# A state-space layer on one core: each pair of states scanned by one instruction of 1024 columns instead of two of 512

## The chip, the core and the metric

One of the eight cores of a Trainium2 chip runs the whole program. Its engines are TensorE (PE, matrix products, with a separate row PEld for its weight loads), VectorE (DVE), ScalarE (ACT), GpSimd (POOL) and SyncE (SP, which here issues the DMAs). Each engine works through its own list of instructions in order and stops at a semaphore until another engine has raised it. The metric is the device time of one execution in microseconds (us), median of the runs.

## What is computed

Two layers follow each other on an input of 2 sequences, 2048 positions, 512 features, in float32. The first is a conditional Mamba layer, the second a linear attention layer. The change lies in the scan of the first:

```
xz = in_proj(layernorm(x) * (1 + scale) + shift);  x_in, z = split(xz)      # 1024 channels each
u  = silu(causal_conv4(x_in));  dt_r, B, C = split(x_proj(u));  dt = softplus(dt_proj(dt_r))
for each position t, channel d, state n (16 of them):
    h[d,n] = h[d,n] * exp(dt[t,d] * A[d,n]) + (dt[t,d] * u[t,d]) * B[t,n]
    y[t,d] = sum_n h[d,n] * C[t,n]
y = (y + u * D) * silu(z);  x = x + gate * out_proj(y)
```

## The kernel before

**Tiling.** The 2 x 2048 positions are cut into 8 chunks c of 512 positions. The 1024 channels are cut into 8 tiles j of 128. A chunk and a tile make a unit, U = 8c + j, 64 of them; a unit has 16 states, so there are 1024 steps s = 16U + pr, with pr the state from 0 to 15. Two neighbouring states make a pair, G = s // 2, 512 of them; g = G % 8 is the pair's place in its unit. The scan runs along the 512 positions, in columns, and is one VectorE instruction for a state.

**The path of one pair.** (1) ACT computes the decays exp(dt * A) of a state (`exps`), 512 columns, into one of four PSUM banks, DA[s % 4]. (2) VectorE, or GpSimd for the pairs in `POOLED`, multiplies dt*u by the B of both states into a buffer hb of 2 x 512 columns (`expand`). Six such buffers go round (R = 6), and an expand waits until TensorE has read the pair six before (semaphore p_y). (3) VectorE scans each state in place (`scan`, line 1094): it waits for the state's decays (a_da) and for the expand (v_tt or g_ex), and counts v_sc up when it is done. (4) ACT copies the pair's last column where a later chunk needs it (`keep_state`), and GpSimd multiplies both states by C (line 1529). (5) TensorE adds up the states over transposed matmuls into PSUM (`nsum`, line 368).

**The order.** All of it is written out by hand: each engine runs a loop over the 1024 steps, and tables say at which (tile j, state pr) an engine puts in the work that belongs to other places: the next unit's softplus ('soft': pr 6 on ACT, behind a copy of the last unit's sums at the same pr 6, `y_copy`), the product with silu(z) (`y_fin`, pr 11 on VectorE), the next chunk's projections, convolution and silu, the last chunk's output projection. ACT runs three steps ahead: in its step s it first does what the tables put there and then `exps(s + 3)`. That call waits until the bank that it overwrites has been scanned, `e.wait_ge(v_sc, s - 3)` in terms of its own s. VectorE's order in an even step is `expand` of the next pair, then the scan of the first state; the second state's scan follows in the odd step. A softplus and a silu each need an activation table of their own, which is loaded by ACT (lines 654 and 890 around a silu, 654 and 754 around a softplus).

**Pooled pairs.** By the tables `EACH` and `OWN`, 114 of the 512 expands are GpSimd's. In the units up to U = 62, where ACT puts in a softplus, the pairs g = 4 and g = 5 are both VectorE's in 42 units, and one of the two is GpSimd's in 21 (mostly j = 2, 6 and 7). In the units with j = 4, one of the pairs g = 1 and g = 2 is GpSimd's; there ACT has a silu of z and one of u at pr 0.

After the 1024 steps the second layer follows, which the change doesn't touch.

## Time and profile before

| | |
|---|---|
| median of 3 runs | 2237.83 us (2236.24 to 2241.0) |
| profiled execution, its own time | 2238.82 us |
| span of the profile | 2237.0 us |
| stretch of the scans, 69 to 1747 us | 1678 us: DVE busy 1642, POOL 1593, PE 1500, ACT 1370 |
| before it and after it | 69 us and 490 us |
| mean granted TensorE clock | 0.974 |

A busy time is the sum of an engine's records. Records of VectorE and ACT overlap a little: the next one begins before the one ahead has ended, so that the distance from start to start, called the pitch here, is shorter than the duration, and it is the pitch that an instruction costs when the queue is full.

### The profile page before, as it was taken

The page shows a single profiled execution, that of the slowest core. Times are in us where ns is not written, and L with a number is a line of the kernel's source. Part 1 is how long each engine was busy: PE and PEld are TensorE (multiplying, and loading weights), DVE is VectorE, ACT ScalarE, POOL GpSimd, SP SyncE. Part 2 cuts the span into 40 slices and gives each one's busy share as a digit, 9 for nine tenths or more (in the row PEclk, how much of TensorE's full clock was granted, in tenths as well). Part 3 has the DMA queues.
Part 4 walks back from the last instruction along what each step waited for, and adds up shares of the span by engine and source line. Part 5 has one row for each costly group of instructions (what it writes and reads, how often), then busy time and mean ns, then how long its engine had stood idle before and what let it go on. Part 6 is the DMA issues. An engine that isn't in the chain of part 4 may idle for free.

```text
span 2237.0 us, 31435 instructions
## 1 busy us (share of the span) xinstructions
PE 2040.1 (91%) x10240; PEld 1320.8 (59%) x10240; DVE 1985.6 (89%) x2245; ACT 1674.5 (75%) x3186; POOL 1744.8 (78%) x1139
## 2 busy tenths in 40 slices
PE   8889989988998999899989988999868899999999
PEld 3355555545555554555555555545545688888878
DVE  4899999989999999999999999999999766666666
ACT  3688797878887888888887889887677455466655
POOL 0599999999999999999999999999999422232225
PEclk9899999999999999999999999999988999999999
DMA  6623342352234143434342351334001211111113
GB/s 219 240 83 95 97 165 67 85 171 85 76 98 176 57 104 81 175 99 99 107 149 66 86 191 56 84 93 179 29 29 55 99 34 36 37 53 62 41 57 132
DMA packets 122592, 220.73 MB, mean 99 GB/s; under 512 B 24317, under 2 KB 39933, under 8 KB 122430
## 3 DMA queue, kind: packets, MB, share of 16 engines
q1 hardware_dynamic: 122430, 218.74, 31.5%
q8 instruction: 82, 1.34, 0.2%
q14 instruction: 80, 0.66, 0.1%
HBM read 171.91 MB, written 17.30 MB: 85 GB/s over the span
## 4 chain that ended last, share of the span: by engine, by line
PE 44%; issue 15%; DVE 14%; POOL 11%; ACT 11%; DMA 3%; SPq 1%; DVEq 0%; POOLq 0%; ACTq 0%
PE ps L516 15%; DVE arena L1094 9%; PE ps L297 9%; POOL arena L1529 8%; PE ps L368 6%; DVE arena L1082 5%; PE ps L358 3%; ACT arena L654 3%; ACT ps L654 3%; PE ps L344 2%; ACT L654 2%; POOL arena L1493 2%; PE ps L324 2%; ACT L754 1%; PE ps L510 1%
## 5 line engine op out<-in xcount | busy, mean ns | idle before, releaser
L1529 POOL TENSOR_TENSOR arena<-arena 128x1024 f32<-128x1024 f32 x512 | 1199.8, 2362 | 97.3 <-ACT arena L654 93.8
L1094 DVE TENSOR_TENSOR_SCAN arena<-ps,arena 128x512 f32<-128x512 f32 x1024 | 1189.3, 1202 | 13.0 <-ACT ps L654 12.0
L654 ACT ACTIVATE ps<-arena 128x512 f32<-128x512 f32 x1087 | 713.2, 677 | 207.7 <-DVE arena L1082 105.6
L368 PEld LDWEIGHTS ps<-keep,arena 128*128 128x128 f32 x4096 | 475.0, 144 | 311.0 <-POOL arena L1529 170.7
L368 PE MATMUL ps<-keep,arena 128*128 128x128 f32 x4096 | 540.8, 281 | 117.9 <-POOL arena L1529 100.0
L1082 DVE TENSOR_TENSOR arena<-ps,arena 128x1024 f32<-128x1024 f32 x398 | 476.7, 1198 | 22.4 <-PE ps L368 18.2
L297 PE MATMUL ps<-arena 128*128 128x512 f32 x1024 | 469.2, 600 | 12.4 <-issue 11.5
L297 PEld LDWEIGHTS ps<-arena 128*128 128x128 f32 x1024 | 188.0, 192 | 229.4 <-issue 228.9
L1493 POOL TENSOR_TENSOR arena<-arena 128x1024 f32<-128x1024 f32 x114 | 269.3, 2362 | 17.2 <-PE ps L368 17.1
L358 PE MATMUL ps<-arena 128*128 128x512 f32 x512 | 238.1, 601 | 1.7 <-DVE arena L1115 1.7
L654 ACT ACTIVATE arena<-ps 128x512 f32<-128x512 f32 (+2 forms) x330 | 168.4, 526 | 77.4 <-PE ps L297 58.2
L654 ACT ACTIVATE arena<-arena 128x2 f32<-128x2 f32 (+6 forms) x678 | 190.8, 300 | 27.3 <-DMA arena<-scr_bc 14.6
L1541 POOL TENSOR_TENSOR arena_c<-arena_c 128x512 f32<-128x512 f32 x32 | 33.4, 1044 | 161.6 <-DVE arena_c L1253 160.4
L358 PEld LDWEIGHTS ps<-arena 128*128 128x128 f32 x512 | 96.1, 196 | 104.4 <-issue 99.8
L654 ACT ACT_TABLE_LOAD x121 | 155.2, 1283 | 2.9 <-PEq L1857 0.7
L324 PE MATMUL ps<-arena 128*64 128x512 f32 x448 | 112.5, 624 | 27.5 <-DMA arena<-arena 27.3
L1423 POOL TENSOR_SCALAR arena_b<-arena_b 128x2 f32<-128x2 f32 x32 | 7.4, 231 | 143.9 <-DVE arena_b L1104 143.7
L654 ACT ACTIVATE arena_c<-arena_c 128x256 f32<-128x256 f32 (+3 forms) x112 | 54.9, 493 | 85.9 <-POOL arena_c L1541 59.4
L654 ACT ACTIVATE arena_b<-ps,keep 128x256 f32<-128x256 f32 x128 | 70.9, 554 | 50.4 <-PE ps L510 41.0
L1213 DVE TENSOR_TENSOR xl<-arena_b,xh 128x256 fp32r<-128x256 f32 x128 | 57.6, 467 | 45.4 <-ACT xh L654 44.6
L1463 POOL TENSOR_TENSOR arena<-arena 128x511 f32<-128x511 f32 (+1 forms) x63 | 80.1, 1272 | 14.4 <-ACT arena L654 11.4
L654 ACT ACTIVATE arena_b<-arena_b 128x512 f32<-128x512 f32 x64 | 48.5, 806 | 50.4 <-POOL arena_b L1428 50.4
(153 smaller groups left out, 2683.4 us busy)
## 6 DMA issues: line engine op xcount, KB each, us to landing
arena<-in_inT SPq DMA_DIRECT2D x184, 256.0 KB, 2.8
arena<-scr_bc SPq DMA_DIRECT2D x80, 512.0 KB, 10.0
arena<-arena SPq DMA_DIRECT2D x224, 128.5 KB, 2.4
arena<-scr_bc SPq DMA_DIRECT2D x48, 511.0 KB, 9.5
arena<-in_x SPq DMA_DIRECT2D x17, 512.0 KB, 3.7
scr_x<-arena SPq DMA_DIRECT2D x32, 256.0 KB, 2.0
arena_b<-scr_x SPq DMA_DIRECT2D x16, 512.0 KB, 3.6
arena_c<-scr_x SPq DMA_DIRECT2D x32, 256.0 KB, 2.9
```

The source lines that it names most:

```text
L297: last = e.matmul(P, W[:, q, :], xnT[c % 2][:, q, :], start=(q == 0), stop=(q == 3))
L324: last = e.matmul(P[64 * h:64 * h + 64, :], W[:, 2 * h + p, 0:64], xt[:, h, 2 * p:2 * p + T], start=(p == 0), stop=(p == 1))
L358: e.matmul(P, u[c % 2][:, q, 128 * n:128 * n + 128], wout[:, q, :], start=(c == NCH - 1 and q == 0 or parts and q == 6), stop=(q == 7 or p ...
L368: last = e.matmul(YP[:, 128 * q:128 * q + 128], hb[G % R][:, i, 128 * q:128 * q + 128], ident, start=(g == 0 and i == 0 and q == 0), stop= ...
L516: last = e.matmul(P, lhs(a, k), rhs(b, k), start=(k == 0 and n == 0), stop=(k == 3 and n == 2))
L654: return e.activation(o_, i_, f, **kw)
L1082: e.tensor_tensor(hb[G % R], DU.unsqueeze(1).broadcast_to([128, GN, T]), Bt[:, GN * g:GN * g + GN, :], MUL).then_inc(v_tt)
L1094: e.tensor_tensor_scan(H, DA[s % 4], H, 0.0, MUL, ADD).then_inc(v_sc)
L1213: e.tensor_tensor(lo[:, f, :], f_bufs[i % 3], hi[:, f, :].bitcast(f32), SUB).then_inc(v_lo)
L1463: e.tensor_tensor(spt[:, lo:T], dt[U % 2][:, lo:T], u[c % 2][:, j, lo:T], MUL).then_inc(g_du)
L1493: e.tensor_tensor(hb[G % R], spt.unsqueeze(1).broadcast_to([128, GN, T]), Bt[:, GN * g:GN * g + GN, :], MUL).then_inc(g_ex)
L1529: e.tensor_tensor(H, H, Ct[:, GN * g:GN * g + GN, :], MUL).then_inc(g_w)
```

## The change

The four decay banks become one PSUM tensor of 4 x 512 columns, so that two neighbouring banks can be read as one row of 1024. A pair's scan is now one instruction (`joint`) over 1024 columns of decays and of hb. So that the second state doesn't start from the last value of the first, the first column of every second bank is set to zero once, at the start (semaphore a_z0), and the decays of odd states are written from column 1 on. A product with zero then cuts the chain; the exact decay of that first column was never used, since the state starts at zero (later chunks add the kept state through B's first column). `JOINT` holds all 64 places, so no pair is left scanned in two. "Slots kept" in the words of the change means that the tables of places, the four banks and the waits of `exps` stay as they are.

```
-        PS = [ctx.enter_context(nc.psum_tensor(f"ps{i}", [128, 512], f32))[:, :] for i in range(8)]
+        decay = ctx.enter_context(nc.psum_tensor("ps_da", [128, 4, 512], f32))
+        PS = [decay[:, i, :] for i in range(4)] + [ctx.enter_context(nc.psum_tensor(f"ps{i}", [128, 512], f32))[:, :] for i in range(4, 8)]
...
+        JOINT = {(0, 0), (0, 1), (0, 2), (0, 3), (0, 4), (0, 5), (0, 6), (0, 7), (1, 0), (1, 1), (1, 2), (1, 3), (1, 4),
...
                 if s >= 4:
                     e.wait_ge(v_sc, s - 3)
-                act(DA[s % 4], dt[U % 2], ACT.Exp, scale=An[:, U % 8, n:n + 1]).then_inc(a_da)
+                lo = s % 2
+                act(DA[s % 4][:, lo:T], dt[U % 2][:, lo:T], ACT.Exp, scale=An[:, U % 8, n:n + 1]).then_inc(a_da)
...
             e.wait_ge(a_A, 2)
+            act(decay[:, 1::2, 0], zero3[:, 0:2], ACT.Identity).then_inc(a_z0)
             exps(0)
...
             def scan(s):
                 U, n = divmod(s, 16)
                 c, j = divmod(U, 8)
-                H = hb[(s // 2) % R][:, s % 2, :]
-                e.wait_ge(a_da, s + 1)
+                joint = (j, n // 2) in JOINT
+                if s == 0:
+                    e.wait_ge(a_z0, 1)
+                e.wait_ge(a_da, s + 2 if joint else s + 1)
...
-                e.tensor_tensor_scan(H, DA[s % 4], H, 0.0, MUL, ADD).then_inc(v_sc)
+                H = hb[(s // 2) % R]
+                if joint:
+                    e.tensor_tensor_scan(flat(H), flat(decay[:, s % 4:s % 4 + 2, :]), flat(H), 0.0, MUL, ADD).then_inc(v_sc, 2)
+                else:
+                    e.tensor_tensor_scan(H[:, s % 2, :], DA[s % 4], H[:, s % 2, :], 0.0, MUL, ADD).then_inc(v_sc)
...
             expand(0)
-            scan(0)
...
-                if s:
+                if s % 2 == 0 or (j, pr) not in JOINT:
                     scan(s)
```

On VectorE, unit 40 from its pair g = 4 to its pair g = 6 stood so before. The rows of line 1082 are expands (of g = 5, 6 and 7), those of line 1094 scans, and line 1115 is `y_fin`:

```order
L1082 TENSOR_TENSOR arena<-ps,arena 128x1024 [waits p_y,g_E0,d_B5]
L1094 SCALAR_TENSOR_TENSOR arena<-ps,arena 128x512 [waits v_tt,a_da] x2
L1082 TENSOR_TENSOR arena<-ps,arena 128x1024 [waits p_y,g_E0,d_B6]
L1094 SCALAR_TENSOR_TENSOR arena<-ps,arena 128x512 [waits v_tt,a_da]
L1115 TENSOR_TENSOR arena<-ps,arena 128x512 [waits a_sz,p_yb]
L1094 SCALAR_TENSOR_TENSOR arena<-ps,arena 128x512 [waits v_tt,a_da]
L1082 TENSOR_TENSOR arena<-ps,arena 128x1024 [waits p_y,g_E0,d_B7]
```

Now the same place reads so; line 1090 is the expand, 1106 the joint scan, 1129 `y_fin`:

```order
L1090 TENSOR_TENSOR arena<-ps,arena 128x1024 [waits p_y,g_E0,d_B5]
L1106 SCALAR_TENSOR_TENSOR arena<-ps_da,arena 128x1024 [waits v_tt,a_da]
L1090 TENSOR_TENSOR arena<-ps,arena 128x1024 [waits p_y,g_E0,d_B6]
L1106 SCALAR_TENSOR_TENSOR arena<-ps_da,arena 128x1024 [waits v_tt,a_da]
L1129 TENSOR_TENSOR arena<-ps,arena 128x512 [waits a_sz,p_yb]
L1090 TENSOR_TENSOR arena<-ps,arena 128x1024 [waits p_y,g_E0,d_B7]
```

Two scans have become one, whose wait on a_da now counts both states, and `y_fin` has moved from between the two scans of pair g = 5 to behind the joint one.

On ACT, the softplus of unit 40 stood so before. The rows that write ps and wait on v_sc are `exps` (of states 7, 8 and, last, 9), 128x2 is `keep_state`, the row that waits on p_y is `y_copy`, the one on p_dt the softplus:

```order
L654 ACTIVATE ps<-arena 128x512 [waits v_sc] x2
L654 ACTIVATE arena<-arena 128x2 [waits v_sc]
L654 ACTIVATE ps<-arena 128x512 [waits v_sc]
L654 ACTIVATE arena<-ps 128x512 [waits p_yb,p_y]
L654 ACT_TABLE_LOAD [waits g_du]
L654 ACTIVATE arena<-ps 128x512 [waits p_dt]
L754 ACT_TABLE_LOAD
L654 ACTIVATE ps<-arena 128x512 [waits v_sc]
```

And now:

```order
L660 ACTIVATE ps_da<-arena 128x512 [waits v_sc]
L660 ACTIVATE ps_da<-arena 128x511 [waits v_sc]
L660 ACTIVATE arena<-arena 128x2 [waits v_sc]
L660 ACTIVATE ps_da<-arena 128x512 [waits v_sc]
L660 ACTIVATE arena<-ps 128x512 [waits p_yb,p_y]
L660 ACT_TABLE_LOAD [waits g_du]
L660 ACTIVATE arena<-ps 128x512 [waits p_dt]
L760 ACT_TABLE_LOAD
L660 ACTIVATE ps_da<-arena 128x511 [waits v_sc]
```

Nothing on ACT has moved: the four instructions still stand between the exponentials of states 8 and 9. Only the odd states are one column shorter. The waits on v_sc keep their numbers, but v_sc now goes up by two at the end of a pair.

## Rows read from the trace of the kernel before

**Rows 1.** Windows: busy time of each engine in the stretch of the scans.

```profile
69.00:1747.00 1678.00, 1500.47 (x6809) 877.67 (x6808) 1642.46 (x1499) 1369.77 (x2558) 1593.25 (x900) 0.97 0.34 105
```

**Rows 2.** VectorE's groups by line, in that stretch: busy, mean ns; idle before.

```profile
L1094 DVE TENSOR_TENSOR_SCAN arena<-ps,arena 128x512 f32<-128x512 f32 x1024 | 1189.3, 1202 | 13.0 <-ACT ps L654 12.0
L1082 DVE TENSOR_TENSOR arena<-ps,arena 128x1024 f32<-128x1024 f32 x397 | 475.5, 1198 | 19.0 <-PE ps L368 18.2 <-POOL arena L1483 0.7
L1115 DVE TENSOR_TENSOR arena<-ps,arena 128x512 f32<-128x512 f32 x63 | 42.0, 666 | 3.5 <-PE ps L381 3.5
```

**Rows 3.** Waits of ACT for VectorE: us in total, times, longest.

```profile
ACT ps L654 <- DVE arena L1082: 105.6, 53, 3.8
ACT ps L654 <- DVE arena L1094: 99.4, 138, 2.6
```

**Rows 4.** Timeline of VectorE, unit 40: start, us, instruction.

```profile
1128.86 2.33 DVE L1094 TENSOR_TENSOR_SCAN arena<-ps,arena 128x512 f32<-128x512 f32 x2
1131.11 1.20 DVE L1082 TENSOR_TENSOR arena<-ps,arena 128x1024 f32<-128x1024 f32 x1
1132.22 2.33 DVE L1094 TENSOR_TENSOR_SCAN arena<-ps,arena 128x512 f32<-128x512 f32 x2
1134.47 1.20 DVE L1082 TENSOR_TENSOR arena<-ps,arena 128x1024 f32<-128x1024 f32 x1
1135.58 2.32 DVE L1094 TENSOR_TENSOR_SCAN arena<-ps,arena 128x512 f32<-128x512 f32 x2
...
1140.07 0.66 DVE L1115 TENSOR_TENSOR arena<-ps,arena 128x512 f32<-128x512 f32 x1
1140.66 1.21 DVE L1094 TENSOR_TENSOR_SCAN arena<-ps,arena 128x512 f32<-128x512 f32 x1
```

**Rows 5.** Timeline of ACT at the softplus of unit 40.

```profile
1130.11 0.69 ACT L654 ACTIVATE ps<-arena 128x512 f32<-128x512 f32 x1 [1.35 <-DVE arena L1094]
1131.20 0.60 ACT L654 ACTIVATE arena<-ps 128x512 f32<-128x512 f32 x1 [0.40 <-PE ps L368]
1131.82 1.28 ACT L654 ACT_TABLE_LOAD   x1
1133.11 0.60 ACT L654 ACTIVATE arena<-ps 128x512 f32<-128x512 f32 x1
1133.72 1.28 ACT L754 ACT_TABLE_LOAD   x1
1135.02 0.69 ACT L654 ACTIVATE ps<-arena 128x512 f32<-128x512 f32 x1
1135.65 0.57 ACT L654 ACTIVATE arena<-arena 128x2 f32<-128x2 f32 x3
```

**Rows 6.** Timeline of VectorE at the softplus of unit 47, where g = 5 is GpSimd's.

```profile
1316.07 3.44 DVE L1094 TENSOR_TENSOR_SCAN arena<-ps,arena 128x512 f32<-128x512 f32 x3
1320.28 1.22 DVE L1094 TENSOR_TENSOR_SCAN arena<-ps,arena 128x512 f32<-128x512 f32 x1 [0.77 <-ACT ps L654]
```

**Rows 7.** Timeline of ACT at the same place: the exponential of state 9.

```profile
1319.56 0.69 ACT L654 ACTIVATE ps<-arena 128x512 f32<-128x512 f32 x1
```

**Rows 8.** Timeline of ACT at the silu of unit 44 (j = 4), between states 2 and 3.

```profile
1226.68 1.28 ACT L654 ACT_TABLE_LOAD   x1
1227.97 0.60 ACT L654 ACTIVATE arena<-ps 128x512 f32<-128x512 f32 x1
1228.46 1.05 ACT L654 ACTIVATE arena<-arena 128x1024 f32<-128x1024 f32 x1
1229.53 1.28 ACT L890 ACT_TABLE_LOAD   x1
1230.83 0.69 ACT L654 ACTIVATE ps<-arena 128x512 f32<-128x512 f32 x1
```

**Rows 9.** Timeline of VectorE at that place: pairs 6, 7, an expand, pairs 0, 1.

```profile
1222.49 4.55 DVE L1094 TENSOR_TENSOR_SCAN arena<-ps,arena 128x512 f32<-128x512 f32 x4
1226.97 1.20 DVE L1082 TENSOR_TENSOR arena<-ps,arena 128x1024 f32<-128x1024 f32 x1
1228.08 4.69 DVE L1094 TENSOR_TENSOR_SCAN arena<-ps,arena 128x512 f32<-128x512 f32 x4
```

More of the change, by code:

```diff
@@ L139, in program @@
             ("ft", "q", "v", "k", "qt", "kt", "kv", "ya", "o"))
-        a_sc, a_A, a_row, a_no, a_xn, a_xh, a_hi, a_e0, a_xq, a_ue, a_du, a_su, a_xd, a_sp, a_sz, a_da, a_st, a_dg, a_x1, a_sm, a_sq = (
-            sem("a_" + n) for n in ("sc", "A", "row", "no", "xn", "xh", "hist", "e0", "xq", "ue", "du", "su", "xd", "sp", "sz",
+        a_z0, a_sc, a_A, a_row, a_no, a_xn, a_xh, a_hi, a_e0, a_xq, a_ue, a_du, a_su, a_xd, a_sp, a_sz, a_da, a_st, a_dg, a_x1, a_sm, a_sq = (
+            sem("a_" + n) for n in ("z0", "sc", "A", "row", "no", "xn", "xh", "hist", "e0", "xq", "ue", "du", "su", "xd", "sp", "sz",
                                     "da", "st", "dg", "x1", "sm", "sq"))
@@ L1159, in _ @@
                     expand(s // 2 + 1)
-                if s:
+                if s % 2 == 0 or (j, pr // 2) not in JOINT:
                     scan(s)
```

4 rows, old and new, of the table JOINT are left out of this document.

## The prediction

> **What bounds the kernel now.** I read the windows first. In the stretch of the scans VectorE is busy for 1642 of 1678 us, GpSimd for 1593, TensorE for 1500, ACT for 1370 [rows 1]. Records overlap a little, so none of these is quite a queue's load, but the order is clear: VectorE sets the pace, GpSimd follows at 95%, ACT has 18% to spare. VectorE's groups by line say what it does there: 1024 scans, 397 expands, 63 `y_fin`; and how little it waits: 12.0 us for decays from ACT, 18.2 and 3.5 us for TensorE, in 1678 [rows 2]. What VectorE is made to do or to wait for therefore lands in the time almost whole. ACT, in turn, waits some 205 us for VectorE in 191 places [rows 3]. The view ascribes about half of it to the expand, but by the program these are `exps`, which wait for a scan to free their bank. So ACT is on average ahead. The timelines show where it is not: at its bursts of table loads.
>
> **What the change takes away.** VectorE's queue gives the price from start to start. Two scans and what lies between them cost 1131.11 - 1128.86 = 2.25 us, an expand of 1024 columns 1.11 us, `y_fin` with 512 columns 0.59 us [rows 4]. The last two are the same operation with one operand in PSUM, so 512 columns cost 0.52 us and what is paid once for an instruction is 1.11 - 1.04 = 0.07 us. Taking that for the scan too, the joint scan costs 2.25 - 0.07 = 2.18 us, and 512 pairs save 36 us. The trace holds no scan of 1024 columns and none across two banks. Bounds: if the second bank or the longer row costs what the merging saves, 2.25 and a gain of 0. At the other end, if the fixed part is all by which a scan's record of 1.202 us [rows 2] exceeds twice 0.52 us, it is 0.16 us, and 82 us are saved. I take 0.07, the nearest row.
>
> The page "VectorE: DVE Perf Modes" of the Trainium skill (section on the TRN2 errata) gives a PSUM-source instruction 120 cycles beside one per element, and says that "a single large tile pays it once". At its 0.96 GHz that would be 0.125 us a pair and 64 us in all, an estimate from that page; the pitch in the rows shows 0.07 us of it, since the queue begins the next instruction before the last has ended.
>
> **What it adds: two banks come free at once, and two must be full at once.** Before, the first state's bank was free a scan earlier than the second's, and the second state's decays were needed a scan later than the first's. Now `exps` of both states of a pair wait for the end of the joint scan two pairs back, and both must be done before the next joint scan on those banks starts. From that end to that start VectorE does an expand, a joint scan and an expand: 1.11 + 2.18 + 1.11 us, less the 0.08 us by which records overlap (2.33 of 2.25), 4.32 us. With one of the expands on GpSimd it is 3.21 us. Within it ACT must do two exponentials and all that the tables put between them.
>
> *The softplus.* At pr 6 the tables put four instructions between the exponentials of states 8 and 9: `y_copy`, a table load of 1.28 us, the softplus, a table load of 1.28 us, from 1131.20 to 1135.02, 3.82 us [rows 5]. The need is 0.05 us from a scan's end (1128.86 + 1.20) to the exponential at 1130.11, 0.63 us for that one (the pitch of 1135.02 to 1135.65), 3.82, 0.69 for the second and 0.03 to the scan: 5.22 us. In the 42 units in which both expands are VectorE's, pair 4 starts 5.22 - 4.32 = 0.90 us late; in the other 21, 5.22 - 3.21 = 2.01 us. Unit 47 shows the second case without a model: the exponential of state 9 ended at 1319.56 + 0.69 = 1320.25 [rows 7], where the scan of state 8 had begun at 1316.07 + 2 x 1.12 = 1318.31 and that of state 9 waited until 1320.28 [rows 6]. A joint scan could not have begun before 1320.28, 1.97 us later than the scan of state 8 did. Together 42 x 0.90 + 21 x 2.01 = 80 us.
>
> *The silu at j = 4, pr 0.* From 1226.68 to 1230.83 ACT is at table loads and two silus, 4.15 us, between states 2 and 3 [rows 8]. The need is 0.05 + 0.63 + 4.15 + 0.69 + 0.03 = 5.55 us. Between pair 7 of the unit before and pair 1 VectorE has one expand and one joint scan (pairs 6 and 7, an expand, pairs 0 and 1 [rows 9]): 3.21 us. Late by 2.34 us in 7 units; in the last chunk, without the silu of u (1.05 us), by 1.29. Together 18 us.
>
> *Other bursts.* Where a burst stands before an even state, ACT meets it while it would wait anyway, and nothing is lost. I didn't walk every place. Units with j = 1, 5 and 6 have further silus, statistics and evacuations within a pair; I allow each of these 24 units one plain lateness of 0.9 us, 22 us, an estimate and the weakest term.
>
> *What takes some of it back.* 12.0 us of waiting for ACT is there already [rows 2] and is part of the 120. VectorE's 22 us of waits for TensorE [rows 2] shrink when it comes later anyway; I take half, 11 us, between 0 and 22.
>
> **What costs nothing.** `y_fin` moves behind the joint scan, one scan later in its unit; its input is rarely late (3.5 us in all [rows 2]) and now less so. Odd exponentials are one column shorter. The one zeroing instruction stands at the start, before the decays that ACT has ready ahead of the first expand. GpSimd, `keep_state` and TensorE wait for the end of a pair as before, and come 36 us sooner or with the late pairs later. SP's queue is untouched, and so is everything after 1747 us.
>
> **The sum.** 80 + 18 + 22 - 12 - 11 = 97 us of waits, less 36 us saved: 61 us more on 2238.82 us, the profiled execution's own time, which stands 1 us above the median of the runs. On the median that is 2299 us, 2.7% slower.
>
> **The rivals.**
> *ACT is far enough ahead, and only the saving remains.* For it: ACT's 205 us of waits for VectorE. Against it: those waits lie outside the bursts, and rows 6 and 7 show a decay ready after the scan ahead of it had begun. It decides where what stands between two exponentials is shorter than 4.32 - 1.40 = 2.92 us (1.81 with a GpSimd expand), and it is 3.82. Then the time would be 2238 - 36 = 2202 us. Chance 0.07.
> *Another queue sets the pace, so that neither term is seen.* GpSimd is at 95% and TensorE at 89% [rows 1]. Then VectorE would be waiting for freed buffers; it does so for 18 us [rows 2], so at most that much could be hidden or kept from it. About 2238 us. Chance 0.04.
> *The fixed part of an instruction is larger*, as a scan's record, not its pitch, would have it: 82 us saved, windows 0.09 us shorter at some 95 places (9 us lost): 2299 - 46 + 9 = 2262 us. The pitch in rows 4 speaks against it. The page of the Trainium skill named above speaks for a part of it: by its 64 us the time would be about 2276 us, an estimate. Chance 0.12.
> *Nothing is taken back and the joint scan saves nothing.* A late joint scan delays GpSimd's multiplication, TensorE's sums and with them the next expands; with a joint scan of 2.25 us the windows grow by 0.07 us (7 us less late): 2238 + 120 - 12 - 7 = 2339 us. For it: GpSimd has only 85 us of slack. Against: six buffers go round. Chance 0.12.
> The forecast itself, 2275 to 2325 us, has 0.65.
>
> **How the numbers follow.** The likeliest case gives 2299 us. The range goes from 2258 us, a little under the case of the larger fixed part, to 2335 us, nearly the worst case; it leaves out the first two rivals and the tails of the others. A measurement of this kernel tells 0.2% from no change, 4.5 us. Faster 0.07, the same 0.04, slower 0.89.
>
> **What the next profile would show.** 512 scans with a pitch of 2.18 us (2.1 to 2.25) in VectorE's timeline, and VectorE's busy time lower by some 60 us, since records overlap. VectorE waiting for ACT at line 1106 about 105 us in some 110 places, where it was 12 us in 25; the longest of about 2 us, in the units with j = 2, 6 and 7 at pair 4 and with j = 4 at pair 1, and of about 0.9 us at pair 4 of the others. ACT's waits for VectorE about as long as before. The stretch of the scans about 1740 us long, and 490 us behind it. The prediction is wrong if ACT's waits for VectorE stand within a pair, ahead of the burst, or if the pitch of the joint scan is far from 2.18 us; and its size is wrong if places other than pairs 4 and 1 hold most of the waiting.

## The result, and the profile after

The change made the kernel slower, as forecast, but by more: 2341.42 us, median of 4 runs (2337.99 to 2342.04), against 2237.83 us before. The ratio is 1.046 [1.0447, 1.0472], 104 us, where 61 us were forecast. The time stands 6 us above the upper end of the range. The profiled execution took 2341.62 us, its span is 2339.8 us.

The windows of the changed kernel, in the stretch of the scans (columns as in [rows 1]):

```profile
67.00:1849.00 1782.00, 1537.29 (x6805) 888.00 (x6806) 1622.53 (x987) 1382.13 (x2558) 1596.17 (x899) 0.95 0.32 99
```

The stretch is 1782 us long instead of 1678; what follows it has kept its 490 us. All of the loss lies here. VectorE is busy 20 us less than before (1622.53, before 1642), yet the stretch is 104 us longer: it waits. (The view counts overlapping records once, so a busy time is less than the sum of the records that was named ahead: 1024 scans of 1.202 us make 1231 us, where [rows 2] has 1189.3.) Its groups by line, in the same stretch, say for whom:

```profile
L1106 DVE TENSOR_TENSOR_SCAN arena<-ps_da,arena 128x1024 f32<-128x1024 f32 x512 | 1161.2, 2278 | 127.5 <-ACT ps_da L660 82.7 <-issue 44.5
L1090 DVE TENSOR_TENSOR arena<-ps,arena 128x1024 f32<-128x1024 f32 x397 | 476.7, 1201 | 31.6 <-PE ps L374 31.5
L1129 DVE TENSOR_TENSOR arena<-ps,arena 128x512 f32<-128x512 f32 x63 | 41.9, 665 | 0.2 <-PE ps L387 0.2
```

Beside [rows 2]: the scans wait 127.5 us where they waited 13.0 us; the expands wait 31.6 us for TensorE where it was 19.0; only `y_fin` waits less, 0.2 us for 3.5. Of the scans' waits 44.5 us are marked "issue", a wait for which the view names no releaser. The timeline shows what they are. VectorE in unit 40, from pair 3 to the expand behind pair 4:

```profile
1193.72 2.27 DVE L1106 TENSOR_TENSOR_SCAN arena<-ps_da,arena 128x1024 f32<-128x1024 f32 x1
1195.92 1.20 DVE L1090 TENSOR_TENSOR arena<-ps,arena 128x1024 f32<-128x1024 f32 x1
1197.04 2.27 DVE L1106 TENSOR_TENSOR_SCAN arena<-ps_da,arena 128x1024 f32<-128x1024 f32 x1
1199.23 1.20 DVE L1090 TENSOR_TENSOR arena<-ps,arena 128x1024 f32<-128x1024 f32 x1
1201.24 2.29 DVE L1106 TENSOR_TENSOR_SCAN arena<-ps_da,arena 128x1024 f32<-128x1024 f32 x1 [0.81 <-issue]
1203.45 1.20 DVE L1090 TENSOR_TENSOR arena<-ps,arena 128x1024 f32<-128x1024 f32 x1
```

and ACT between the exponentials of states 8 and 9 of that unit:

```profile
1196.03 0.69 ACT L660 ACTIVATE ps_da<-arena 128x512 f32<-128x512 f32 x1 [1.88 <-DVE arena L1106]
1196.66 0.58 ACT L660 ACTIVATE arena<-ps 128x512 f32<-128x512 f32 x1
1197.26 1.28 ACT L660 ACT_TABLE_LOAD   x1
1198.55 0.60 ACT L660 ACTIVATE arena<-ps 128x512 f32<-128x512 f32 x1
1199.17 1.28 ACT L760 ACT_TABLE_LOAD   x1
1200.46 0.69 ACT L660 ACTIVATE ps_da<-arena 128x511 f32<-128x511 f32 x1
```

The joint scan that begins at 1193.72 frees both banks at its end. 0.04 us later, at 1196.03, ACT begins to fill them, and the burst of the tables stands between the two exponentials, as in [rows 5]. The second one ends at 1201.15 and the joint scan of pair 4 begins at 1201.24. VectorE had nothing else from 1200.43 on. From freeing to scanning it is 5.25 us (the prediction had 5.22). The lateness in the row is 0.81 us; counted as the prediction counts, from where the scan would have begun with the usual overlap of 0.08 us, it is 0.89 us (0.90). So a wait marked "issue" here is a wait for ACT all the same, as the end of the exponential just ahead of the scan shows.

ACT in turn waits far longer for the scans, and TensorE longer ahead of line 303. Rows of the changed kernel's waits (engine, line, waited for: us in total, times, longest):

```profile
ACT ps_da L660 <- DVE arena L1106: 266.7, 257, 4.7
...
ACT ps L660 <- DVE arena L1090: 55.7, 55, 1.6
...
PE ps L303 <- issue: 30.5, 12, 3.8
```

The same wait of TensorE before, where the line was 297:

```profile
PE ps L297 <- issue: 11.5, 8, 2.1
```

The first row of [rows 3] is not `exps`, as the prediction took it to be. ACT has a second write into PSUM that waits for VectorE, `du_copy`, the copy of the next unit's dt*u, which waits until the last expand of its unit has read the old one. It writes ps in both kernels, and the exponentials of the changed kernel write ps_da, so the rows above keep the two apart: `du_copy` waits 55.7 us (105.6 before), the exponentials 266.7 us (99.4 before).

Walked record by record, from the end of the instruction ahead to the start of each scan, the waits for decays rose from 16.5 to 137.6 us (+121). Waits of the expands and of `y_fin` rose together from 25.3 to 33.8 us (+8.5). A pair in two scans took 2.245 us from start to start where nothing waited (the median; [rows 4] have 2.25 twice). The joint scan takes 2.197 us (2.20, 2.19 and 2.21 in the rows of unit 40 above). So merging saves 0.048 us a pair, 25 us in all. 121 + 8.5 - 25 = 104.5 us, and from the first scan's start to the last one's end the trace has 1781.5 instead of 1677.9 us, +103.6. The expectations below reckon with 2.235, 2.182 and 0.053 us, which is some 2 us more in all.

### The profile page after: what moved, and what is told of

It is laid out like the page before. It is cut to its first block, busy times and chain, and to the rows that moved or that the text cites. A ratio compares the mean times of both kernels' runs of the same rounds, so it can differ in the third digit from the quotient of the medians.

```text
span 2339.8 us, 30412 instructions
## 1 busy us (share of the span) xinstructions
PE 2075.1 (89%) x10240; PEld 1330.2 (57%) x10240; DVE 1966.6 (84%) x1733; ACT 1687.1 (72%) x3187; POOL 1748.7 (75%) x1139
## 4 chain that ended last, share of the span: by engine, by line
PE 38%; ACT 24%; DVE 17%; issue 12%; POOL 5%; DMA 3%; SPq 1%; DVEq 0%; ACTq 0%; POOLq 0%
DVE arena L1106 11%; PE ps_da L522 8%; ACT ps_da L660 7%; PE ps L522 7%; ACT arena L660 7%; PE ps L303 6%; PE ps L374 5%; ACT L660 4%; DVE arena L1090 4%; POOL arena L1542 4%; PE ps L364 3%; ACT L760 2%; PE ps L350 2%; PE ps L330 2%; ACT L898 2%
## 5 line engine op out<-in xcount | busy, mean ns | idle before, releaser
L1106 DVE TENSOR_TENSOR_SCAN arena<-ps_da,arena 128x1024 f32<-128x1024 f32 x512 | 1161.2, 2278 | 127.5 <-ACT ps_da L660 82.7
L660 ACT ACTIVATE ps_da<-arena 128x512 f32<-128x512 f32 (+2 forms) x1025 | 677.4, 682 | 269.4 <-DVE arena L1106 266.7
L303 PE MATMUL ps<-arena 128*128 128x512 f32 x1024 | 481.2, 612 | 31.9 <-issue 30.5
L1090 DVE TENSOR_TENSOR arena<-ps,arena 128x1024 f32<-128x1024 f32 x398 | 477.8, 1201 | 35.2 <-PE ps L374 31.5
L303 PEld LDWEIGHTS ps<-arena 128*128 128x128 f32 x1024 | 191.0, 196 | 258.3 <-issue 258.0
L364 PE MATMUL ps<-arena 128*128 128x512 f32 x508 | 252.9, 636 | 2.7 <-DVE arena L1129 2.7
L660 ACT ACTIVATE arena<-ps 128x512 f32<-128x512 f32 (+2 forms) x330 | 168.0, 525 | 61.6 <-PE ps L303 45.6
L660 ACT ACTIVATE arena<-arena 128x2 f32<-128x2 f32 (+6 forms) x678 | 190.6, 299 | 26.0 <-DMA arena<-scr_bc 14.5
L364 PEld LDWEIGHTS ps<-arena 128*128 128x128 f32 x508 | 99.3, 204 | 111.2 <-issue 105.8
L1554 POOL TENSOR_TENSOR arena_c<-arena_c 128x512 f32<-128x512 f32 x32 | 33.5, 1046 | 161.7 <-DVE arena_c L1266 160.5
L330 PEld LDWEIGHTS ps<-arena 128*64 128x64 f32 x448 | 29.5, 140 | 98.4 <-issue 50.4
```

The source lines that it names most:

```text
L303: last = e.matmul(P, W[:, q, :], xnT[c % 2][:, q, :], start=(q == 0), stop=(q == 3))
L330: last = e.matmul(P[64 * h:64 * h + 64, :], W[:, 2 * h + p, 0:64], xt[:, h, 2 * p:2 * p + T], start=(p == 0), stop=(p == 1))
L364: e.matmul(P, u[c % 2][:, q, 128 * n:128 * n + 128], wout[:, q, :], start=(c == NCH - 1 and q == 0 or parts and q == 6), stop=(q == 7 or p ...
L660: return e.activation(o_, i_, f, **kw)
L1090: e.tensor_tensor(hb[G % R], DU.unsqueeze(1).broadcast_to([128, GN, T]), Bt[:, GN * g:GN * g + GN, :], MUL).then_inc(v_tt)
L1106: e.tensor_tensor_scan(flat(H), flat(decay[:, s % 4:s % 4 + 2, :]), flat(H), 0.0, MUL, ADD).then_inc(v_sc, 2)
```

## The experiments

Each was timed beside the kernel before on one chip, and each ratio is to that kernel, which took 2238 to 2239 us each time. "Unit", "pair" and "pr" are as ahead; all idle times are of VectorE's groups by line.

### Half of it each: banks freed in pairs, banks wanted in pairs

Both keep 1024 scans. The first frees the two banks of a pair only when the second is scanned:

```
-                e.tensor_tensor_scan(H, DA[s % 4], H, 0.0, MUL, ADD).then_inc(v_sc)
+                last = e.tensor_tensor_scan(H, DA[s % 4], H, 0.0, MUL, ADD)
+                if s % 2:
+                    last.then_inc(v_sc, 2)
```

> The kernel before with one half of the added wait: two scans, but the first no longer counts, and the second counts for both, so that two banks come free at once at the pair's end. Each scan still waits for its own decays only. By the prediction's windows a second scan may come 1.12 us later than a joint one: softplus late by 0 us in 42 units, by 0.9 in 21, silu at j = 4 by 1.2 in 8, less the 12 us there were: theory A 2245 to 2265 us. Rival B: most of the loss, above 2290 us.

Measured: 2273.77 us, 1.0159 [1.0143, 1.0174], a little over what the forecast's theory expected; the scans wait 38.0 us. The other half lets the first scan of a pair wait for both decays:

```
-                e.wait_ge(a_da, s + 1)
+                e.wait_ge(a_da, s + 2 - s % 2)
```

> The kernel before with the other half: two scans, each counting for itself, but the first waits for the decays of both states. By the trace of before the second decay was ready after the first scan's start by 0.2 us in the 42 plain units, by up to 2 us in the 21 with a GpSimd expand, by 1.2 us at the silu of j = 4: theory A 2260 to 2285 us. Rival B: little, under 2250 us, since the banks still come free one by one.

Measured: 2268.64 us, 1.0149 [1.0121, 1.0176], as that theory expected.

```profile
L1094 DVE TENSOR_TENSOR_SCAN arena<-ps,arena 128x512 f32<-128x512 f32 x1024 | 1191.4, 1206 | 53.3 <-ACT ps L654 53.0
L1082 DVE TENSOR_TENSOR arena<-ps,arena 128x1024 f32<-128x1024 f32 x398 | 477.6, 1200 | 15.7 <-PE ps L368 11.8 <-DMA arena<-scr_bc 3.9
```

Each half alone costs a third, +36 and +31 us, with nothing merged. Together they are some 67 us, and the change has 130 us of waits more (121 + 8.5). Pair 4 makes most of the difference: the scans wait 19 us there in the first run and 33 us in the second, 88 us in the changed kernel. The windows say why: where both expands are VectorE's, one half alone leaves ACT one scan more, 4.32 + 1.12 = 5.44 us, which the softplus burst's 5.22 us still fits; only both halves together make the window too short there. In the places with an expand on GpSimd it is too short with either.

### The order on ACT

If the second exponential stands ahead of the burst, the burst no longer lies within a pair. In even steps `exps(s + 3)` goes before the tables' work, in the changed kernel (e1) and, with the same lines, in the kernel before (e2):

```
+                ahead = s % 2 == 0 and pr != AT["copy"]
+                if ahead and s + 3 < NS:
+                    exps(s + 3)
...
-                if s + 3 < NS:
+                if s + 3 < NS and not ahead:
```

> The changed kernel, but in even steps (all but pr 12) ScalarE does the exponential of step s + 3 before the work that the tables put there, so that nothing stands between the two exponentials of a pair. Theory A (the loss is the work that stands within a pair): VectorE's waits for ScalarE at the joint scan fall from 127 us to under 30, the saving of the merged scans is left, and the time is 2205 to 2230 us. Rival B (with two banks freed at a time ScalarE lacks lead wherever its bursts stand): waits stay above 80 us and the time above 2300 us. Rival C (the coarser steps of the joint scan hold up GpSimd and TensorE, which is why VectorE's waits for them rose from 22 to 35 us): waits for ScalarE go, but the time stays at 2250 to 2285 us.

Measured: 2273.74 us, 1.0157 [1.0142, 1.0172].

```profile
L1109 DVE TENSOR_TENSOR_SCAN arena<-ps_da,arena 128x1024 f32<-128x1024 f32 x512 | 1158.8, 2278 | 41.8 <-ACT ps_da L660 23.5 <-issue 17.7
L1093 DVE TENSOR_TENSOR arena<-ps,arena 128x1024 f32<-128x1024 f32 x398 | 479.5, 1205 | 49.7 <-PE ps L374 42.6 <-DMA arena<-scr_bc 3.9 <-POOL arena L1499 3.1
```

The waits at pair 4 are gone and 68 of the 104 us with them. What is left stands at pairs 2 (19.6 us), 5 (18.8) and 1 (9.2), and the expands wait more for TensorE. The expected time was missed. It lies where rival C had it, and the expands' waits rose as that rival has it, but 41.8 us of waits for decays are left, where it expected next to none.

> The kernel before (two scans of 512 a pair) with the same order on ScalarE as in the run above. Theory A: VectorE waited only 12 us for ScalarE, so there is at most that to win: 2225 to 2240 us. Rivals B and C expect the same; the run is the base for what the joint scan alone is worth where ScalarE is in time (theory A: about 27 us, from pitches of 2.182 us after and 2.235 us before for a pair).

Measured: 2259.89 us, 1.0096 [1.0081, 1.0111], which was missed too. The scans wait 6.1 us, the expands 39.4, `y_fin` 18.3: the order alone costs 22 us, and the waits that grew are those for TensorE. That the later copies and the softplus hold TensorE up is likely, but not shown by this run. Beside it the joint scan costs 14 us.

Then the order at the softplus alone was changed: `y_copy`, the exponential of state 9, the softplus.

```
+                if pr == AT["soft"] and s + 3 < NS:
+                    exps(s + 3)
...
-                if s + 3 < NS:
+                if s + 3 < NS and pr != AT["soft"]:
```

> The changed kernel with one move: at pr 6 the second exponential comes ahead of the softplus and its table loads, but behind the copy of the last unit's sums (y_copy), which keeps its place. The need between the exponentials falls from 3.82 to 0.6 us. Theory D (what exponentials first in all even steps cost beside what it won, 22 us in the kernel before, was TensorE waiting for the later y_copy): pair 4's 88 us of waits go, the expand's waits for TensorE stay at 35 us or under, 2245 to 2265 us, faster than with decays first everywhere. Rival F (it was the later softplus that held up GpSimd and TensorE): expand waits rise to 45 us or more and the time is 2265 us or more.

Measured: 2292.23 us, 1.0242 [1.0221, 1.0263]. Pair 4 waits no more, but pair 5 does (33.7 us, 4.9 before the edit) and the expands too (45.1 us). The expected time was missed, and the numbers are the rival's: the burst now stands between the exponentials of states 9 and 10, begins only when state 9 has its bank, and what comes after it is late. So a burst between two pairs is not free either.

Next the softplus moved to pr 5, ahead of state 8, and its product on TensorE to pr 2, except in tiles j = 7:

```
+        soft_at = lambda U: AT['soft'] if U % 8 == 7 else 5
...
-                    if U + 1 < NU and pr == AT["dt"]:
+                    if U + 1 < NU and pr == (AT["dt"] if U % 8 == 7 else 2):
...
-                if U + 1 < NU and pr == AT["soft"]:
+                if U + 1 < NU and pr == soft_at(U):
```

> The changed kernel with the softplus an odd step earlier (pr 5, its product on TensorE at pr 2; tiles j = 7 keep theirs), so that its table loads stand between two pairs; y_copy stays at pr 6. Theory A: pair 4's waits fall from 88 us to under 25 (those of j = 7, 13 us, stay), nothing comes later on TensorE: 2245 to 2270 us. Rival B (a burst costs wherever it stands): waits of 60 us or more at pairs 4 and 3, above 2290 us.

Measured: 2350.82 us, 1.0506 [1.0486, 1.0525]. Pair 4 falls from 88 to 41 us, but other pairs and `y_fin` (19 us) wait instead, and ACT waits 89.6 us for TensorE's line 304 (45.6 for the same line in the changed kernel). The time is the rival's. The edit moved a product and the life of its bank as well as the burst, so it doesn't tell the two apart. With nine of the 64 places scanned in two beside it:

```
+        JOINT = {(j, p) for j in range(8) for p in range(8)} - {(1, 2), (5, 2), (6, 2), (7, 4), (1, 5), (4, 1), (7, 1), (3, 7), (6, 7)}
...
```

> The softplus at pr 5 and a JOINT of 55 of the 64 places: two scans at pair 2 of j = 1, 5, 6, pair 4 of j = 7, pair 5 of j = 1, pair 1 of j = 4 and 7 and the pairs two ahead of these. Theory A: what remained of the waits in the run above falls to some 35 us, 23 us are saved by joint scans: 2225 to 2245 us, on the level of the kernel before or a little under it. Rival E: 2255 us or more.

Measured: 2310.41 us, 1.0323 [1.0301, 1.0345], a miss. None of these places of the softplus rescues the joint scan.

### Joint only in some places

Pairs 2 and 4 of all tiles and five more places are scanned in two, 43 of 64 jointly:

```
+        JOINT = {(j, p) for j in range(8) for p in range(8)} - {(j, p) for j in range(8) for p in (2, 4)} - {(1, 5), (4, 1), (7, 1), (3, 7), (6, 7)}
...
```

> The changed kernel with a JOINT of 43 of the 64 places: two scans of 512 again at pairs 2 and 4 of every tile, pair 5 of j = 1, pair 1 of j = 4 and 7 and the pairs two ahead of these. Theory A (a pair is late where work stands between its two exponentials): the waits for ScalarE fall from 138 us to about 40, the saving is 0.053 us at 344 pairs, 18 us: 2235 to 2260 us. Rival E (the joint scans around hold ScalarE back in the same way, so the waits move to the neighbours): above 2280 us.

Measured: 2247.95 us, 1.0044 [1.0029, 1.0058]. The waits follow the places: 93 of the 104 us are gone, as expected. The joint scans wait 9.8 us, the single ones 22.9. Then only 27 places, those that had shown no waits:

```
+        JOINT = {(j, p) for j in range(8) for p in (0, 3, 6, 7)} - {(1, 0), (5, 0), (6, 0), (3, 7), (6, 7)}
...
```

> The changed kernel with a JOINT of 27 of the 64 places, those at which neither the pair nor the one two behind it was late: pairs 0, 3, 6 and 7, without pair 0 of j = 1, 5, 6 and pair 7 of j = 3 and 6. The saving is 0.053 us at 216 pairs, 11 us; the waits for ScalarE stay within 10 us of the kernel before. Theory A: 2226 to 2238 us. Rival E (joint scans cost their neighbours more than they save wherever they stand): 2242 us or more.

Measured: 2241.83 us, 1.0015 [1.0006, 1.0024], no gain, and just short of what the rival asked for. Its joint scans wait 0.0 us, but the single scans wait more than before the change, at pair 4 18.7 us where it was 10.7. 216 merges should save 216 x 0.048 = 10 us, and more than that is waited elsewhere. Why the single pairs wait more is not shown by this run.

### The burst taken out

An Exp in the softplus's place needs no table loads, so that the four instructions become two (the logarithm is left out); the same edit was made in the changed kernel (e12) and in the kernel before (e13):

```
-                act(dt[U % 2], BG[bank_of["dt", U]], ACT.Softplus).then_inc(a_sp)
-                e.preload_act_table_set("natural_log_exp_and_others")
+                act(dt[U % 2], BG[bank_of["dt", U]], ACT.Exp).then_inc(a_sp)
...
```

> The changed kernel with an exponential in place of the softplus, so that its two table loads (2.57 us) are gone from between the exponentials of states 8 and 9; it leaves out the softplus's logarithm, everything else is the same. The need at pair 4 falls from 5.22 to 2.65 us, under both windows. Theory A: no wait at pair 4; 88 us of waits less and a stretch shorter by about that, 2240 to 2265 us, waits left at pairs 1 and 2 (45 us). Rival B (paired banks cost lead wherever ScalarE is busy): more than 20 us of waits move to pairs 5 to 7, above 2275 us.

Measured: 2244.37 us, 1.0027 [1.0016, 1.0038].

```profile
L1105 DVE TENSOR_TENSOR_SCAN arena<-ps_da,arena 128x1024 f32<-128x1024 f32 x512 | 1160.0, 2279 | 45.7 <-ACT ps_da L660 42.9 <-issue 2.6
```

97 us of the 104 go with the loads, and pair 4 keeps 2.7 us of its waits, as expected. Of these 97 us the kernel before gains 13 as well, as the next run shows, so 84 of the 104 us are what the burst costs the joint scan. Of all runs this shows most plainly that the softplus burst is the main cause; e17 below says the same with a whole softplus.

> The kernel before with the same exponential in place of the softplus. It is the base for the run above: VectorE waited 11 us at pair 4, so theory A expects 2220 to 2235 us; the joint scan then costs 15 to 35 us where the softplus is no matter, from the waits at pairs 1 and 2 less 27 us of saving. If VectorE does not set the pace there (rival G: TensorE and GpSimd do), the run stays at 2235 us or more.

Measured: 2225.05 us, 0.9945 [0.993, 0.996]; the scans wait 1.3 us. Even without that burst the joint scan costs 19 us (2244.37 - 2225.05): the other bursts' waits, 44 us, still outweigh the 25 us saved.

### The copy of the state

`keep_state` stands behind the exponential in even steps. Ahead of the tables' work it would free hb sooner, if that is what TensorE and the expands wait for:

```
+                if s % 2 == 0 and s > 0 and kept((s // 2 - 1) // NG):
+                    keep_state(s // 2 - 1)
...
-                if s % 2 == 0 and s > 0 and kept((s // 2 - 1) // NG):
-                    keep_state(s // 2 - 1)
```

> The changed kernel with the copy of the state that is kept (keep_state, 0.19 us) ahead of the tables' work in even steps, where it stood behind it and behind the exponential; GpSimd's multiplication of a pair waits for it. It asks why VectorE's waits for TensorE rose by 12 us where they were expected to fall. Theory H: GpSimd came late behind ScalarE's bursts (its waits for ScalarE rose from 94 to 132 us) and TensorE behind it; the expand's waits fall from 35 to 25 us or less and the time by 10 us or more. Rival I: they come from TensorE's own bursts at the end of tiles j = 6 and 7 and stay; the time stays within 5 us of 2341 us.

Measured: 2347.03 us, 1.0485 [1.0471, 1.05]. The expands' wait for TensorE, 33.5 us, is no shorter than the 31.5 us of the changed kernel. GpSimd's multiplication did come sooner (without one long wait at the start it waits 73 us for ACT in the changed kernel and 45 us here), so `keep_state` is not what the expands wait for. Theory H fails; the time is 6 us above the changed kernel's, just outside what the rival allowed.

### A softplus without its two loads

Softplus is log(1 + exp(x)), and both parts are had in the table that the decays use:

```
-                act(dt[U % 2], BG[bank_of["dt", U]], ACT.Softplus).then_inc(a_sp)
-                e.preload_act_table_set("natural_log_exp_and_others")
+                act(dt[U % 2], BG[bank_of["dt", U]], ACT.Exp).then_inc(a_s1)
+                e.wait_ge(a_s1, U + 1)
+                act(dt[U % 2], dt[U % 2], ACT.Ln, bias=1.0).then_inc(a_sp)
...
```

This was run with all pairs scanned in two (e16), all jointly (e17), and with 52 of 64 places joint (e15):

```
+        JOINT = {(j, p) for j in range(8) for p in range(8)} - {(4, 1), (7, 1), (3, 7), (6, 7), (1, 2), (5, 2), (6, 2), (1, 0), (5, 0), (6, 0), (2, 4), (2, 2)}
...
```

> The kernel before with the softplus written so: the base for the run above. Without the logarithm it took 2225 us; the logarithm adds 0.7 us to ScalarE in a unit, behind which little waits: 2222 to 2232 us by every theory.

Measured: 2226.84 us, 0.996 [0.9947, 0.9974]. The softplus's two loads were nearly all that ACT made the scans wait for: 1.3 us are left of 13.0 [rows 2].

```profile
L1096 DVE TENSOR_TENSOR_SCAN arena<-ps,arena 128x512 f32<-128x512 f32 x1024 | 1187.0, 1201 | 1.3 <-ACT ps L655 0.7
L1084 DVE TENSOR_TENSOR arena<-ps,arena 128x1024 f32<-128x1024 f32 x398 | 476.6, 1197 | 19.4 <-PE ps L369 11.7 <-POOL arena L1485 5.3 <-DMA arena<-scr_bc 2.4
...
L1117 DVE TENSOR_TENSOR arena<-ps,arena 128x512 f32<-128x512 f32 x64 | 42.7, 666 | 7.7 <-PE ps L382 7.7
```

> The changed kernel, all pairs joint, with the softplus written so. Need at pair 4: 1.4 + 0.6 + 1.3 = 3.3 us, under the plain window of 4.32 and at the pooled one of 3.21. Theory A: as without the logarithm (2244 us) and up to 5 us more, 2242 to 2252 us, 15 to 25 us over single scans with the same softplus.

Measured: 2242.06 us, 1.0015 [1.0006, 1.0024]; the scans wait 43.2 us. With the short burst the joint scan costs 15 us, much as in e12 and e13.

```profile
L1108 DVE TENSOR_TENSOR_SCAN arena<-ps_da,arena 128x1024 f32<-128x1024 f32 x512 | 1159.6, 2276 | 43.2 <-ACT ps_da L661 40.8 <-issue 2.2
L1092 DVE TENSOR_TENSOR arena<-ps,arena 128x1024 f32<-128x1024 f32 x398 | 478.1, 1201 | 19.4 <-PE ps L375 13.2 <-DMA arena<-scr_bc 4.2 <-POOL arena L1498 1.5
```

The expands wait no longer here than with single scans (19.4 us in both), though `y_fin` stands behind the joint scan.

> The softplus written as an exponential and a logarithm of 1 + it, both in the table set that is loaded anyway, so that 1.3 us stand at that place and not 3.82, and a JOINT of 52 of the 64 places, without those that were late for other bursts and the pairs two ahead of them. The saving is 0.053 us at 416 pairs, 22 us. Theory A (VectorE sets the pace, and the saving shows once no pair is late): 2203 to 2218 us, some 15 us under the same softplus with single scans. Rival G (freed from ScalarE's bursts, VectorE meets TensorE and GpSimd, which take the saving): within 6 us of the run with single scans.

Measured: 2221.53 us (2219.72 to 2224.22), 0.9932 [0.992, 0.9944], a few us slower than theory A expected, 5.3 us under e16, and the fastest kernel of the study.

```profile
L1104 DVE TENSOR_TENSOR_SCAN arena<-ps_da,arena 128x1024 f32<-128x1024 f32 x416 | 943.3, 2275 | 8.8 <-issue 4.4 <-ACT ps_da L657 4.3
L1088 DVE TENSOR_TENSOR arena<-ps,arena 128x1024 f32<-128x1024 f32 x398 | 478.1, 1201 | 23.0 <-PE ps L371 18.3 <-DMA arena<-scr_bc 2.8 <-POOL arena L1494 1.6
L1106 DVE TENSOR_TENSOR_SCAN arena<-ps_da,arena 128x512 f32<-128x512 f32 x192 | 223.9, 1202 | 9.9 <-ACT ps_da L657 9.4
```

Against e16 the stretch from the first scan's start to the last one's end is 3.4 us shorter. 416 joint scans save 416 x 0.048 = 20 us, the scans wait some 17 us more by these rows (8.8 + 9.9 against 1.3) and 20 us record by record, and expands and `y_fin` 2 us less. By this account waits eat almost all of the merge's saving. The time alone can't tell theory A from rival G, since 5.3 us are within the 6 us that the rival allowed. The rows speak against it: what takes the saving are waits for decays, while the waits for TensorE and GpSimd, which rival G named, are no longer than in e16.

### `y_fin` ahead of the joint scan

In the changed kernel TensorE stands still ahead of line 303, and the buffers of VectorE's expands come free late. The prediction had costed the new place of `y_fin` at nothing. VectorE at the end of unit 39 in the changed kernel:

```profile
1175.29 2.28 DVE L1106 TENSOR_TENSOR_SCAN arena<-ps_da,arena 128x1024 f32<-128x1024 f32 x1
1177.49 0.67 DVE L1129 TENSOR_TENSOR arena<-ps,arena 128x512 f32<-128x512 f32 x1
1178.07 1.21 DVE L1090 TENSOR_TENSOR arena<-ps,arena 128x1024 f32<-128x1024 f32 x1
1179.20 2.28 DVE L1106 TENSOR_TENSOR_SCAN arena<-ps_da,arena 128x1024 f32<-128x1024 f32 x1
1183.78 1.22 DVE L1090 TENSOR_TENSOR arena<-ps,arena 128x1024 f32<-128x1024 f32 x1 [2.30 <-PE ps L374]
```

and TensorE in those microseconds:

```profile
1173.82 0.60 PE L387 MATMUL ps<-keep,arena 128*128 128x128 f32 x4
1178.26 4.51 PE L303 MATMUL ps<-arena 128*128 128x512 f32 x6 [3.83 <-issue]
1182.60 1.91 PE L374 MATMUL ps<-keep,arena 128*128 128x128 f32 x16
```

`y_fin` ends at 1178.16, and only then TensorE begins the projection at 1178.26, into the bank that `y_fin` has read. TensorE has been idle 3.83 us. Seven more of the twelve waits at line 303, six of them in tiles j = 7 and one in j = 6, end 0.10 us behind a `y_fin` in the same way; the eight make 28.7 of the 30.5 us. TensorE's six products of line 303 stand ahead of those that empty the expand's buffer (line 374), and VectorE waits 2.30 us for them. To undo it, `y_fin` goes between the expand and the joint scan of pr 10:

```
-                if pr == AT["yf"] and U > 0:
-                    y_fin(U - 1)
...
+                if pr == 10 and U > 0:
+                    y_fin(U - 1)
```

> The changed kernel with y_fin between the expand and the joint scan of pr 10, about a scan earlier than in the kernel before and two earlier than in the changed one. Theory J (the joint scan put y_fin behind it, the PSUM bank that y_fin reads comes free a scan later, the projection that takes this bank on TensorE starts later, and the sums queued behind it free VectorE's buffers later): the expand's waits fall from 35 to 24 us or less, TensorE's unexplained waits ahead of the projections from 30 to under 15, and the time by 8 to 15 us, 2326 to 2334 us. Rival K (those waits come from the late joint scans and softplus themselves): expand waits and time stay, 2337 us or more.

Measured: 2337.05 us (2328.57 to 2339.34), 1.044 [1.0419, 1.0461], some 4 us less than the changed kernel (1.046 [1.0447, 1.0472]). The intervals overlap, so a gain is not shown, and the time is rival K's.

```profile
L1106 DVE TENSOR_TENSOR_SCAN arena<-ps_da,arena 128x1024 f32<-128x1024 f32 x512 | 1162.0, 2280 | 127.4 <-ACT ps_da L660 82.5 <-issue 44.5
L1090 DVE TENSOR_TENSOR arena<-ps,arena 128x1024 f32<-128x1024 f32 x398 | 477.5, 1200 | 16.7 <-PE ps L374 13.1 <-DMA arena<-scr_bc 3.5
...
L1129 DVE TENSOR_TENSOR arena<-ps,arena 128x512 f32<-128x512 f32 x64 | 43.9, 686 | 15.7 <-PE ps L387 15.7
```

The waits did what theory J says: the expands wait 16.7 us (35.2 in the whole changed kernel), and TensorE's wait at line 303 falls from 30.5 to 15.3 us. But `y_fin` is now too early for its own input and waits 15.7 us, so that little or nothing is won. The same edit in e15:

> The same move in the fastest kernel so far (softplus by exponential and logarithm, 52 of 64 places joint, 2221.5 us): theory J has the expand's 23 us of waits fall to 15 or less, 2210 to 2218 us, clearly under the single scans with that softplus (2226.8 us). Rival K: 2219 to 2224 us.

Measured: 2242.18 us, 1.0025 [1.0013, 1.0036], 21 us slower than e15 and outside what either theory expected.

```profile
L1088 DVE TENSOR_TENSOR arena<-ps,arena 128x1024 f32<-128x1024 f32 x398 | 477.6, 1200 | 10.7 <-PE ps L371 7.1 <-DMA arena<-scr_bc 3.0
...
L1127 DVE TENSOR_TENSOR arena<-ps,arena 128x512 f32<-128x512 f32 x64 | 44.1, 689 | 42.1 <-PE ps L384 42.1
```

`y_fin` waits 42.1 us where it waited 2.5. Of the three places tried, the one between the two scans, where it stood before, was the best for both: late enough for its input, early enough for its bank. One joint scan of 2.2 us no longer offers it.

## Why the prediction was right in kind and too small

| term of the sum | forecast, us | measured, us |
|---|---|---|
| waits at pair 4 | 80 | 87.8, in 63 places |
| waits at pair 1 | 18 | 25.9, in 20 places |
| waits at other pairs | 22 | 23.9 (pairs 2 and 5) |
| waits for decays there already | -12 | -16.5 |
| waits of expands and `y_fin` | -11 | +8.5 |
| merging | -36 | -25 |
| together | +61 | +104.6; +103.6 from the first scan's start to the last one's end |

**What bounds, and what the joint scan does to it: right.** VectorE sets the pace, the two banks make a common window, and the burst of the softplus doesn't fit in it. The window and the need, 4.32 and 5.22 us, stand in the rows of unit 40 to a few hundredths (a lateness of 0.89 us, forecast 0.90). 63 places were forecast for pair 4 and 63 wait. Without the two loads of the softplus the joint scan costs 19 us (e12, e13) or 15 us (e16, e17) and not 104.

**"VectorE's 22 us of waits for TensorE shrink when it comes later anyway; I take half": this step failed most**, and with it "`y_fin` moves behind the joint scan ... costs nothing". The term has the wrong sign, 20 us of the 43 us that the sum falls short. Waits of expands and `y_fin` did not fall by 11 us but rose by 8.5. The prediction looked at what `y_fin` waits for, and there it was right (3.5 us became 0.2), and not at who waits for `y_fin`: its bank is the one that TensorE's next projection takes. e18 shows that link, since 18 us of the expands' waits go with the place of `y_fin`. The places fit in part: the expands' waits at the end of tiles j = 7, where this projection stands, rose from 1.9 to 12.7 us, those at the end of tiles j = 6 from 12.6 to 17.0. But the new place alone does not make the rise. `y_fin` stands behind the joint scan in e12 and e17 too, and without the softplus's loads the expands wait 23.3 and 19.4 us there, against 19.8 and 19.4 us with single scans (e13, e16).

Nor does a late VectorE always give nothing back. In e4, where the banks come free one by one and `y_fin` keeps its place, the scans wait more, and the waits of expands and `y_fin`, walked record by record, fall from 25 to 14.5 us, as the prediction had it. With the banks freed in pairs (e3) they rise to 31 us, `y_fin` being where it was, and in the changed kernel to 33.8. So it takes the late pairs, with the banks freed in pairs, to turn the sign. How much of the rise the place of `y_fin` adds to that was not told apart.

**The waits for decays: right at the bursts that were walked, 13 us too small in all, and one step of it wrong.** Pair 4 has 8 us more than forecast, pair 1 8 us more, most of it (6.8 us) in tiles j = 7 that were not walked. The bursts that were only guessed at 22 us came out at 23.9, at pairs 2 (19.0) and 5 (4.9), mostly in j = 5 and 6. The other pairs have none to speak of. That the guess came so near is luck. It was made for work within a pair, but in tiles j = 5 and 6 at pair 2 (13.8 us), and in tiles j = 7 at pair 1, the silu stands ahead of the pair's even state, where the prediction says that "nothing is lost". Unit 45 (j = 5), ACT from the silu's first load to the two exponentials of pair 2:

```profile
1326.41 1.28 ACT L660 ACT_TABLE_LOAD   x1
1327.71 0.60 ACT L660 ACTIVATE arena<-ps 128x512 f32<-128x512 f32 x1
1328.20 1.05 ACT L660 ACTIVATE arena<-arena 128x1024 f32<-128x1024 f32 x1
1329.27 1.28 ACT L898 ACT_TABLE_LOAD   x1
1330.56 1.30 ACT L660 ACTIVATE ps_da<-arena 128x512 f32<-128x512 f32 x2
```

and VectorE's joint scan of pair 2:

```profile
1331.95 2.29 DVE L1106 TENSOR_TENSOR_SCAN arena<-ps_da,arena 128x1024 f32<-128x1024 f32 x1 [1.34 <-ACT ps_da L660]
```

Both exponentials follow the burst without a gap, and the scan is late all the same. e8, with the softplus between states 9 and 10, shows it too (33.7 us at pair 5).

**The saving: right in kind, 11 us too large.** What is paid once for an instruction, taken from the expand as 0.07 us, is 0.048 us for the scan. The pair of scans was read rightly (2.25 us; the median is 2.245), and the joint scan's pitch is 2.197 us (2.181 to 2.208), where 2.18 was forecast. The Trainium skill, page "VectorE: DVE Perf Modes" (section on the TRN2 errata), would have 0.125 us a pair and 64 us in all, an estimate from that page. The trace does not bear it out for instructions that follow each other without a gap: there the merge saves 25 us. VectorE's busy time fell by 20 us and not by the 60 that were to show, since the view counts the overlaps once.

**The rivals.** ACT is not far enough ahead: with single scans the softplus's loads are all that it lacks (e13, e16), with joint scans 43 us of waits stay without them (e17). Of the 205 us of waits that spoke for this rival only 99 were the exponentials'. That another queue sets the pace is against the rows: the loss stands in VectorE's waits for decays, and they, not waits for TensorE or GpSimd, take the saving in e15. A larger fixed part falls with the pitch. The last rival, that nothing is taken back and nothing saved, gave 2339 us and is nearest in number. Its first half holds, since nothing was taken back; its second does not, since 25 us are saved, and the waits that were there before grew by 8.5 us more. That the number fits is chance.

**Open.** Why the softplus at pr 5 (e9) is no better than at pr 6 is not settled. The moved product and its bank were changed with it, and the two were not told apart; that a burst ahead of an even state costs too (unit 45) may be a part of it. Nor is it settled why single pairs wait more beside joint ones in e14, nor what holds TensorE up in e1 and e2. In the changed kernel TensorE was busy for 37 us more in the stretch of the scans (1537 for 1500) at a granted clock of 0.95 instead of 0.97; whether that has a part in the expands' waits was not told apart.

## What to carry to other kernels

Where one consumer instruction takes the place of two, its buffers are freed and wanted in pairs: compare the time from the end of one to the start of the next on the same buffers with the longest burst that the producer has between two fills, and scan singly, or shorten the burst, where it doesn't fit. A burst between two pairs counts as well, though it leaves the pair's two fills together. Price the saving by the pitch of the queue, not by the records' length. For an instruction that shifts place, ask who waits for the buffer that it frees, and not only what it waits for.

## What was not expected of the hardware

One VectorE scan reads across two PSUM banks at no charge that shows: 512 of them with a pitch of 2.197 us, 0.048 us less than two scans of one bank each took together (2.245 us).

The larger surprise is the price of ACT's table loads here. The softplus as Exp and Ln is one instruction longer and two loads shorter. ACT in unit 40 of e16, from the exponential of an even state to that of the next:

```profile
1121.02 0.69 ACT L655 ACTIVATE ps<-arena 128x512 f32<-128x512 f32 x1 [1.43 <-DVE arena L1096]
1121.65 0.58 ACT L655 ACTIVATE arena<-ps 128x512 f32<-128x512 f32 x1
1122.38 0.60 ACT L655 ACTIVATE arena<-ps 128x512 f32<-128x512 f32 x1 [0.15 <-PE ps L353]
1123.01 0.63 ACT L655 ACTIVATE arena<-arena 128x512 f32<-128x512 f32 x1
1123.55 0.68 ACT L655 ACTIVATE ps<-arena 128x512 f32<-128x512 f32 x1
```

The burst is 1.90 us long (1121.65 to 1123.55) where it was 3.82 us [rows 5], and the kernel before gains 0.4% by it alone, though ACT is not its bound.
